# A two-layer attention block over 32 graphs: first loads in another order, and the largest sums of the weights found by TensorE and VectorE instead of GpSimd

## The reference

```python
h = jnp.maximum(_layernorm(x, axis=-1), 0.0)           # x: (32, 256, 384)
x = x + _L0_gnn_ref(h, Wq, bq, Wk, bk, Wv, bv, Wf, bf, adj)
h = jnp.maximum(_layernorm(x, axis=-1), 0.0)
x = x + _L1_gnn_ref(h, adj, W, b, w_src, w_dst, H_w, H_b)
# L0: masked softmax attention, 6 heads of 64:
#   probs = softmax(q k^T / 8 + where(adj, 0, -9e15));  (probs v) @ Wf + bf
# L1: graph attention, 12 heads of 32:
#   h = feat @ W;  attn = leaky(tanh(h) w_src + (tanh(h) w_dst)^T), -999 where not adj
#   elu(softmax(attn) @ h + b), mixed with feat by a sigmoid gate (feat @ H_w.T + H_b)
```

## Time and profile before

| | us |
|---|---|
| median of three runs | 1360.45 |
| the profiled execution | 1360.17 |
| its span, first to last instruction | 1358.3 |
| PE busy | 1293.0 (95%) |
| ACT busy | 1252.5 (92%) |
| DVE busy | 1213.5 (89%) |
| POOL busy | 903.3 (66%) |

### The profile page before, as it was taken

One profiled execution on the slowest core, in us unless ns is written; L12 is line 12 of the kernel. 1 busy time (PEld: TensorE's weight loads), 2 busy tenths in 40 slices (PEclk: granted clock), 3 DMA queues, 4 the chain that ended last, 5 costly groups with the idle time before them and its releaser, 6 DMA issues.

```text
span 1358.3 us, 33510 instructions
## 1 busy us (share of the span) xinstructions
PE 1293.0 (95%) x10502; PEld 905.9 (67%) x10502; DVE 1213.5 (89%) x4457; ACT 1252.5 (92%) x3731; POOL 903.3 (66%) x1106
## 2 busy tenths in 40 slices
...
DMA packets 29839, 33.75 MB, mean 25 GB/s; under 512 B 10464, under 2 KB 29664, under 8 KB 29664
## 3 DMA queue, kind: packets, MB, share of 16 engines
...
...
## 4 chain that ended last, share of the span: by engine, by line
PE 89%; ACT 2%; DVE 1%; issue 1%; POOL 1%; POOLq 0%; DVEq 0%; ACTq 0%
PE job L462 26%; PE pt L535 20%; PE job L476 13%; PE unit L511 7%; PE job L597 7%; PE job L553 7%; PE unit L526 3%; PE job L450 3%; PE job L605 2%; PE job L458 1%; ACT p L715 1%; PE job L587 1%; DVE unit L945 0%; POOL prod L1098 0%; ACT pT L723 0%
## 5 line engine op out<-in xcount | busy, mean ns | idle before, releaser
L715 ACT ACTIVATE p<-y,min 128x256 f32<-128x256 f32 x768 | 396.1, 542 | 1.5 <-DVE min L951 1.4
L535 PE MATMUL pt<-ident,p 128*128 128x128 f32 x2304 | 355.6, 280 | 9.7 <-ACT p L715 5.2
L945 DVE SCALAR_TENSOR_TENSOR unit<-unit,s,dst 128x256 f32<-128x256 f32 x768 | 334.8, 481 | 9.4 <-DVE min L951 0.5
L535 PEld LDWEIGHTS pt<-ident,p 128*128 128x128 f32 x2304 | 265.9, 142 | 86.5 <-issue 43.6
L462 PE MATMUL job<-w,h 128*128 128x384 f16 x1728 | 301.8, 326 | 0.7 <-DVE h L844 0.6
L951 DVE CUSTOM_DVE_ANT_0 y<-unit,mask 128x256 f32<-128x256 f32 x768 | 291.0, 415 | 0.0
L1076 POOL TENSOR_SCALAR p<-p,rec 128x256 f32<-128x256 f32 x384 | 188.3, 507 | 88.3 <-DVE rec L886 82.6
L462 PEld LDWEIGHTS job<-w,h 128*128 128x128 f16 x1728 | 166.5, 98 | 104.7 <-issue 0.8
L723 ACT ACTIVATE pT<-pt 128x512 f32<-128x512 f32 x384 | 232.1, 626 | 1.2 <-PE pt L535 1.1
L672 ACT ACTIVATE p<-y,min 128x256 f32<-128x256 f32 x384 | 191.2, 505 | 36.6 <-PE pt L535 28.1
L476 PE MATMUL job<-h,w 128*128 128x256 f16 x1728 | 216.7, 274 | 1.4 <-DVE h L844 1.4
...
## 6 DMA issues: line engine op xcount, KB each, us to landing
xb<-in_x_dram SPq DMA_DIRECT2D x32, 384.0 KB, 3.4
out_dram<-y SPq DMA_DIRECT2D x32, 384.0 KB, 2.5
...
```

What stands on the lines that cost most here:

```text
L535: last = nc.tensor.transpose(pt_ps[u % 2][:, (2 * hh + kt) * P:(2 * hh + kt + 1) * P], probs[:, u % 3, hh, kt * P:(kt + 1) * P], ident[:])
L715: last = op(p1[:, u % 3, hh, :], y1[:, u % YB, hh, :], ACT.Exp, bias=min1[:, u, hh:hh + 1], scale=-1.0, accum_out=sum1[:, t, h:h + 1])
L945: V.scalar_tensor_tensor(leaky[:, hh * T:(hh + 1) * T], bank[:, hh * T:(hh + 1) * T], s8[par][:, t, h:h + 1], dst5[:, c % 2, hh, :], ALU.a ...
```

## The change

GpSimd's three `partition_all_reduce` operations go. In their place, for each pair of weights, TensorE transposes the two columns of sums to two rows in PSUM (`sums_transposed`), VectorE takes the maximum of each row and copies it over 128 columns of a zeroed tile (`largest_sums`), and TensorE multiplies that tile by two columns of the identity, which puts the two maxima on all 128 partitions (`largest_spread`); `scales` reads them from PSUM. The loads go in another order: the three bias columns ahead of batch 0's x, then WF and WV, then the bias rows, then WH and WG. The one-time work is spread: the sums and high parts of WF and WV into turn -1, those of WH and WG at V 1 and EXP0 5, their low parts at PV0 1 of turn 0, `scales(2)` after SCORES0 3, `gate_bias` after AGGREGATE1 of turn 0, the scaling of src_row and dst_row after K 2, the making of `pick` after NORM1 of turn 0, the bias row's matmuls ahead of V 0.

```diff
@@ sync: order of the first loads
-            small = [
-                (bv_c[:], bv), (bq_c[:], bq), (bk_c[:], bk),
...
             def load_others():
-                for dst, src in small:
-                    sp.dma_start(dst, src).then_inc(s_small, 16)
-                for w in (WF, WV, WH, WG):
-                    load_weight(w)
+                load_weight(WF)
+                load_weight(WV)
+                for dst, src in rows:
+                    sp.dma_start(dst, src).then_inc(s_rows, 16)
+                load_weight(WH)
+                load_weight(WG)
             load_weight(WQ)
             load_weight(WK)
+            for dst, src in columns:
+                sp.dma_start(dst, src).then_inc(s_columns, 16)
@@ tensor
+            def value_bias_row():
+                pe.wait_ge(s_w[WF], 16)
+                pe.wait_ge(s_bvw, 1)
+                for c in range(NC):
+                    last = mm(pt_ps[0][:, 0:H], bv_w[:, c, :], stage[WF][:, c, :], start=c == 0, stop=c == NC - 1)
+                last.then_inc(s_row, 1)
+            sums = pt_ps[1]
+            def sums_transposed(pair):
+                pe.wait_ge(s_wsum, 2 * pair + 2)
+                nc.tensor.transpose(sums[0:2, pair * P:(pair + 1) * P], wsum[:, 2 * pair:2 * pair + 2],
+                                    ident[:]).then_inc(s_sums_t, 1)
+            def largest_spread(pair):
+                pe.wait_ge(s_largest, 2 * pair + 2)
+                mm(sums[:, NC * P + 2 * pair:NC * P + 2 * pair + 2], largest_row[:], ident[:, 0:2],
+                   start=True, stop=True).then_inc(s_spread, 1)
+            pe.wait_ge(s_pool_const, 4)
+            sums_transposed(0)
+            largest_spread(0)
...
             def v(b, par, t):
+                if b.ref == 0 and t == 0:
+                    value_bias_row()
...
             def pt0(b, par, u):
+                if b.ref == 0 and u == 1:
+                    pe.wait_ge(s_setup, SCALES_DONE[2])
@@ scalar
-            for w in (WF, WV):
-                sum_weight(w)
-            for w in (WQ, WK, WF, WV):
+            for w in (WQ, WK):
                 high_weight(w)
-            for w in (WH, WG):
-                sum_weight(w)
...
             def exp0(b, par, u):
...
+                if b.ref == 0 and u == 5:
+                    high_weight(WH)
+                    high_weight(WG)
@@ vector
+            def largest_sums(pair):
+                dve.wait_ge(s_sums_t, pair + 1)
+                V.reduce_max(largest[0:2, pair:pair + 1], pt_ps[1][0:2, pair * P:(pair + 1) * P],
+                             AX_X).then_inc(s_largest, 1)
+                dve.wait_ge(s_largest, 2 * pair + 1)
+                V.tensor_copy(largest_row[0:2, :],
+                              largest[0:2, pair:pair + 1].broadcast_to([2, P])).then_inc(s_largest, 1)
             def first_weights():
+                largest_sums(0)
+                scales(0)
                 low_weight(WQ)
                 low_weight(WK)
...
-            scales(0)
-            scales(1)
...
             def aggregate1(b, par, _):
                 aggregate(b, 1, "STATS1", 1)
+                if b.ref == 0:
+                    gate_bias()
...
                 if b.ref == 0 and p == 0:
-                    scales(WH // 2)
+                    scales(1)
                 if b.ref == 0 and p == 1:
-                    low_weight(WH)
-                    low_weight(WG)
-                    gate_bias()
+                    low_weight(WF)
+                    low_weight(WV)
+                if b.ref == 0 and p == 2:
+                    bias_row()
+                    scale_rows()
...
             def pv0(b, par, p):
...
+                if b.ref == 0 and p == 1:
+                    low_weight(WH)
+                    low_weight(WG)
@@ gpsimd
-            def largest_sums(pair):
-                at = slice(2 * pair, 2 * pair + 2)
-                pool.wait_ge(s_wsum, 2 * pair + 2)
-                G.partition_all_reduce(wsum_all[:, at], wsum[:, at], P, RMAX).then_inc(s_wsum_all, 1)
...
             def norm1(b, par, _):
...
+                if b.ref == 0:
+                    make_pick()
```

112 lines of the change are left out of this document (68 added, 44 removed).

## The result

| us | before | after | forecast |
|---|---|---|---|
| median (range; 11 runs each) | 1360.45 (1359.67 to 1361.76) | 1357.89 (1356.49 to 1359.36) | 1352.7 |
| span of the profiled execution | 1358.3 | 1355.6 | |
| Q 0 of batch 0 | 31.63 | 16.86 | 16.8 |
| SCORES0 0 | 47.71 | 33.70 | 33.7 |
| OUT0 | 66.80 | 53.14 | 53.9 |

The ratio is 0.998 with a 95% interval of 0.9971 to 0.9989: faster, clear of the noise but by 0.2% only, 2.56 us where 7.7 were forecast. The page of the kernel after gives the same picture of the bound as the earlier trace rows: busy time, the granted clock in 40 slices, then the chain.

What follows compares the result with a forecast made beforehand. TensorE's instructions bound the loop, so only its entry moves: 14.8 to Q 0, less 0.8, 1.1, 3.1 for pick and 2.1 for exclusion, gives 7.7 us, hence 1352.7, range 1349.4 to 1356.2.

Steps and rivals of the forecast that it cites:

- The bound, the turn, and the sign: Loop: TensorE's work sets each turn, 39.74 us and unchanged; an earlier entry makes the kernel faster, chance 0.95.
- Rival (d): Loop: new offsets between engines lengthen each turn, 0.25 us a turn cancelling the gain, over 0.34 measurably slower; chance 0.02.
- GpSimd's gaps: GpSimd before the first reduction, normalisation and mask: idle gaps, some 7 us, read as program code changes, would go.
- Rival (c): GpSimd at the start: the gaps stay, normalisation at 12.2 instead of 9.7, time 1354.6; chance 0.07.
- To Q 0: Start to Q 0 of batch 0 on TensorE: starts at 16.8 instead of 31.63, gain 14.8 us.
- to SCORES0: From Q 0 to SCORES0 0 on VectorE: starts at 33.7 instead of 47.71, gain 14.0 us.
- to OUT0: From SCORES0 0 to OUT0 of batch 0: stretch 20.2 us instead of 19.1, OUT0 at 53.9, gain 12.9.
- To SCORE_PROD: OUT0 to SCORE_PROD of batch 0 on GpSimd: pick delays it to 71.0, taking turns with VectorE to 73.1.
- the exclusion: gate_bias beside NORM1 and pick: two-input VectorE operations and GpSimd's SBUF reads exclude each other, 2.1 us on GpSimd's chain.
- If SCORE_PROD starts x us earlier, everything behind it does.: Behind SCORE_PROD of batch 0: sums, DST_T and TensorE's unbroken work pass its whole lead on to the end.
- (a): End of turn 0: no exclusion, selects and gate_bias run side by side, gain 9.8, time 1350.6; chance 0.2.
- (b): New turn 0: TensorE's lower clock stays, as it is still mostly waiting; 1356.2 with the long bound; chance 0.2.

Runs made afterwards that it cites:

- e6: The kernel after with GpSimd's partition_all_reduce put back in the three places, the new order kept: 1381.92 us, ratio 1.0148.
- e1: The kernel after with the three selects that make pick moved back to GpSimd's start: 1354.0 us, ratio 0.9949.
- e9: The kernel after with extra matmuls, whose result nothing reads, in TensorE's gaps of turns 0 and 1, into a free bank: 1352.64 us, ratio 0.9941.
- e11: e8 with the scaling of src_row and dst_row moved from K 2 of batch 0 to K 0 of batch 1: 1348.7 us, ratio 0.9915.
- e2: The kernel after with gate_bias moved from behind AGGREGATE1 of batch 0 to behind K 2 of batch 1: 1354.11 us, ratio 0.9955.
- e3: The kernel after with the low parts of WH and WG moved from PV0 1 to behind K 1 of batch 1: 1354.32 us, ratio 0.9955.
- e10: e8 with extra matmuls, whose result nothing reads, in its shorter TensorE gaps: 1347.13 us, ratio 0.9901.
- e8: The kernel after with pick behind NORMP0 5, low parts of WH and WG behind K 1 of batch 1, gate_bias in two pieces: 1347.54 us, ratio 0.9905.

## Why the forecast was right and wrong

*The bound, the turn, and the sign.* Right: the loop passes on what enters it. Rival (d) is out: 39.75 a turn.

*GpSimd's gaps*. Right, and shown by e6 as well: the gaps belong to partition_all_reduce. Rival (c) is out: nmean came 0.18 us behind the aggregate's end.

*To Q 0, to SCORES0, to OUT0.* 16.8, 33.7 and 53.9 forecast, 16.86, 33.70 and 53.14 measured. x was there by 7.9. The step to SCORES0 hid two errors of opposite sign. The chain to the end of QK 0 was 0.9 us shorter than counted (32.69 against about 33.6): the 18 matmuls of Q 0 and K 0 took 3.54 where 4.0 were counted, and the steps behind them were shorter too. And dst_row's scaling, held beside RES_ROW, cost 1.0.

*To SCORE_PROD: the step that failed.* The forecast took GpSimd's chain for the last one. It charged the exclusion to that chain, 2.1 us, and left VectorE's and TensorE's at 70.1, although its own bound for what VectorE can lose, 4 us, would have put that chain at 74.1, later than 73.1. And it charged the clock nothing; every duration of that stretch was taken from rows at the full rate. Measured, the wait that ended last was the one for tanh: VectorE lost 2.6 us in gate_bias, and the lower clock cost 1.6 to 1.7 from OUT0's start to the end of the statistics (6.6 instead of 4.95) and 2.2 from HEADS' start to SCORE_PROD (6.02, where e1 has 3.79). With OUT0's lead of 0.8 these terms give 70.1 - 0.8 + 1.6 + 2.6 + 2.2 = 75.7, and 75.63 was measured. GpSimd's chain ended at 73.0, as forecast, but by luck: it too started 0.8 early and had the 1.6 of OUT0, and the exclusion took about 1 of it (NORM1 1.79 for 1.31, the selects 5.37 for 4.94) and not 2.1.

The exclusion was counted for operations with two inputs only, and that was wrong: a cast took 1.59 for 0.36. The Trainium skill (SBUF — State Buffer, "Who interferes with whom") says that copy, cast and tensor_scalar can enter modes that use the port pair shared with GpSimd, when their operands meet certain conditions, and so can contend with it. The traces agree: the cast here, the copies of bv in e1 (0.50 to 1.85), and dst_row's scaling (1.87, where src_row's took 0.35). The prediction had used the sentence on two inputs alone.

*"If SCORE_PROD starts x us earlier, everything behind it does."* Wrong by 1.6 us for the third fall and by 0.8 in the last batches. The first is a cost at a place where TensorE never waits, which no reading of waits finds.

*The rivals.* (a) is out: gate_bias took 7.7. (b), the lower clock, had 0.2 and is the one whose mechanism was seen, but at other places than it named: not QK 1 and the bias row (1.14 and 2.10 us), but OUT0, HEADS and the start of turn 1. Its argument against, that no gap as long as 4.86 is left, rested on one row; in after OUT0 fell behind 3.12. The three falls lengthened their stretches by 1.6, 2.2 and 1.6 us. That is 5.4 in all and near the 5.1 that are missing, but the two sums are not the same: at SCORE_PROD, 2.5 behind the forecast, the clock's 3.8 stand beside VectorE's 2.6, with a lead and GpSimd's slack taken off. What e9 shows is that the clock's part by itself is worth 4.5 to 5.2 us. What e1 shows is that without the exclusion in gate_bias the gap ahead of HEADS is 1.94 instead of 4.42, and that HEADS then ran at the full rate.

What stays open is why a fall sits where it does. OUT0 stood behind a gap of 3.12 or 3.13 in four kernels: it took 4.76 or 4.77 in after, e1 and e11, and 3.08 in e2. QK 1 of batch 0 stood behind a gap of 1.74 us in all of the following: it took 2.08 in e1 and e9, 1.92 in e2, and 1.13 to 1.14 in after, e3 and e10. DST_T stood behind 1.00 in after, e3, e8, e1 and e11, and only in the first three a fall followed. So the gap ahead does not decide alone, and since the traces are of one execution each, the share of an edit in a fall that went away can't be told from one trace. That not every execution falls in the same places is the likely reason why the eleven runs of after spread over 2.9 us; this was not traced.
